# Half of each gated row turned by a DMA transpose, the outer products two steps behind the inner ones

## The reference

```
for _ in range(LOOPS):
    z_norm = _rmsnorm(z, norm_w)
    scores = softmax(z_norm @ router_w)
    topk_vals, topk_idx = top_k(scores, 2)          # 2 of 8 experts, gates normalised to sum 1
    for e in range(E):                              # E = 8, D = 256, F = 512
        h = silu(z_norm @ w1[e]) * (z_norm @ w3[e])
        mixed = mixed + cw[:, e:e+1] * (h @ w2[e])
    z = z + mixed
```

## Time and profile before

| what | value |
|---|---|
| median of three runs | 1050.6 us |
| the profiled execution | 1050.72 us, its span 1049.0 us, mean granted clock 0.989 |
| attention, up to the first tile | about 343 us |
| 142 tiles, gate of the first to gate of the last | 354.70 to 1023.06 us |
| an undisturbed tile | 4.35 us |
| a tile with a combine step beside it | 5.62 us |
| after the last tile's gate | 25.9 us |

### The profile page before, as it was taken

How to read it: one execution, slowest core, us unless ns; L and a number is a source line. 1 busy time by engine, 2 the same in 40 slices (tenths; PEclk the granted TensorE clock), 3 DMA queues, 4 the chain that set the end, 5 groups by cost and what they waited for, 6 DMA issues and landing times.

```text
span 1049.0 us, 22711 instructions
## 1 busy us (share of the span) xinstructions
PE 987.4 (94%) x7246; PEld 678.7 (65%) x7246; DVE 690.5 (66%) x1497; ACT 574.7 (55%) x1122; POOL 579.5 (55%) x755
## 2 busy tenths in 40 slices
PE   7999997989999899999999999999999999999991
...
GB/s 315 370 68 31 38 32 22 1 6 21 15 26 16 67 107 125 87 69 101 91 109 167 132 98 139 88 106 181 112 111 117 96 91 92 170 173 119 143 187 130
DMA packets 153818, 109.26 MB, mean 104 GB/s; under 512 B 100992, under 2 KB 140544, under 8 KB 153728
## 3 DMA queue, kind: packets, MB, share of 16 engines
...
...
## 4 chain that ended last, share of the span: by engine, by line
PE 69%; DVE 9%; POOL 7%; DMA 6%; ACT 4%; issue 3%; SPq 0%; another core or an unknown queue 0%; POOLq 0%; ACTq 0%; DVEq 0%
PE psum_s L930 32%; PE psum_o L2336 16%; PE psum_s L2325 6%; DMA arena<-arena 4%; PE psum_s L1758 3%; PE psum_t L1753 2%; PE psum_t L764 2%; PE psum_o L1804 2%; POOL arena L1057 2%; DVE arena L1489 1%; DMA arena<-in_rope 1%; PE psum_o L1799 1%; PE psum_o L1811 1%; PE psum_s L1735 1%; PE psum_t L2300 1%
## 5 line engine op out<-in xcount | busy, mean ns | idle before, releaser
L930 PE MATMUL psum_s<-w_all,arena 128*128 x1704 | 392.0, 380 | 4.6 <-issue 1.9
L1980 POOL DMA_INDIRECT token_rows<-arena,result_row_of_row x142 | 147.1, 1036 | 296.5 <-ACT arena L2089 291.2
L930 PEld LDWEIGHTS psum_s<-w_all,arena 128*128 128x128 f16 x1704 | 157.8, 98 | 185.2 <-issue 10.9
L2336 PE MATMUL psum_o<-w_all,arena 128*128 x1704 | 209.4, 273 | 9.1 <-DVE arena L2264 8.2
L915 DVE SCALAR_TENSOR_TENSOR arena<-psum_s,gate_scale,arena 128x512 f32<-128x512 f32 x142 | 106.5, 750 | 161.1 <-ACT arena L909 80.6
L2336 PEld LDWEIGHTS psum_o<-w_all,arena 128*128 128x128 f16 x1704 | 164.7, 98 | 54.1 <-issue 15.4
L2264 DVE TENSOR_TENSOR arena<-psum_s,arena 128x512 f16<-128x512 f32 x142 | 97.8, 689 | 132.3 <-ACT arena L2082 114.2
L2089 ACT ACTIVATE arena<-psum_o 128x256 f32<-128x256 f32 x142 | 54.3, 383 | 216.8 <-PE psum_o L2336 214.1
L891 POOL DMA_INDIRECT arena<-sorted_rows,token_of_row x142 | 139.9, 986 | 49.3 <-issue 40.2
L909 ACT ACTIVATE arena<-psum_s,silu_scale 128x512 f32<-128x512 f32 x142 | 97.6, 687 | 108.1 <-PE psum_s L930 56.6
L2082 ACT ACTIVATE arena<-psum_s 128x512 f16<-128x512 f32 x142 | 84.7, 597 | 33.1 <-PE psum_s L2325 22.9
...
## 6 DMA issues: line engine op xcount, KB each, us to landing
...
arena<-sorted_rows,token_of_row POOLq DMA_INDIRECT x142
token_rows<-arena,result_row_of_row POOLq DMA_INDIRECT x142
...
```

The source lines that it names most:

```text
L930: last = nc.tensor.matmul(bank, e_xT[:, u, lx * DC + c, :], w_split[:, bass.ds(e * EW + at, FF)], start=(q == 0), stop=(q == 3 * DC - 1))
L1980: nc.gpsimd.indirect_dma_start(rows, bass.IndirectOffsetOnAxis(ap=targets[:, at : at + 1], axis=0), y_row[:, u, :], None).then_inc(s_sent[ ...
L2336: last = nc.tensor.matmul(psum_e, hT[:, lh, c, :], w_split[:, bass.ds(e * EW + at, D)], start=(q == 0), stop=(q == 3 * FC - 1))
```

## The change

- The gated row is now made in two halves (`gate`, two operations of 256 columns, the second half of the columns first). The first half is turned by TensorE as before, with two transposes in place of four. The second half is split in the row layout (`half_hi` on ScalarE, `half_lo` on VectorE) into the single buffer `h_split`, and turned by a DMA transpose from SyncE's queue (`turn_half`) into one of two buffers, `hT[1]` or `hT[2]`.
- `outer` stands two steps behind: in step n TensorE does the first half of `inner(n)`, `turn_h(n-1)`, the second half of `inner(n)`, work beside, and `outer(n-2)`. With it `h_hi`, `h_lo`, `y_copy` and `send` are those of n-2.
- The first half of the turned row has one PSUM bank and one buffer, `hT[0]`. So `turn_h(n)` waits for `h_lo(n-1)`, and `h_hi(n-1)` waits for `outer(n-2)`.
- On ScalarE `half_hi(n)` stands behind the work beside the tile and ahead of `y_copy(n-2)`; `h_hi(n-1)` and `silu(n+1)` follow.
- `x_pair` and `y_row` have two buffers in place of three, and `plans` moves most beside work of passes 1 to 3 by one step. One of the closing sums that stood beside a tile (`SUMMED` 6 to 4 tiles of rows) now stands behind the last tile.

The diff, cut to its core:

```diff
@@ -791,12 +791,13 @@
         z_early = [take(2 * D)]
         assert used[0] <= tab_at, used[0]
         used[0] = tab_at
-        x_pair = take(UNROLL * D).bitcast(F16).rearrange("p (u l d) -> p u l d", u=UNROLL, l=2)
+        x_pair = take(2 * D).bitcast(F16).rearrange("p (u l d) -> p u l d", u=2, l=2)
         e_xT = take(UNROLL * D).bitcast(F16).rearrange("p (u g t) -> p u g t", u=UNROLL, g=2 * DC)
         silu_a = take(FF)
         h_row = take(FF)
-        hT = take(2 * FF // 2).bitcast(F16).rearrange("p (l c t) -> p l c t", l=2, c=FC)
-        y_row = take(UNROLL * D).rearrange("p (u d) -> p u d", u=UNROLL)
+        hT = [take(FF // 2).bitcast(F16).rearrange("p (l c t) -> p l c t", l=2, c=FC // 2) for _ in range(3)]
+        y_row = take(2 * D).rearrange("p (u d) -> p u d", u=2)
+        h_split = take(FF // 2).bitcast(F16).rearrange("p (l c) -> p l c", l=2)
...
         LAST = ((0, 4), (4, 8), (8, 12), (12, 14), (14, NT))
-        LAST_LOAD, LAST_SUM = LOW_DONE + 2, LOW_DONE + 4
+        LAST_LOAD, LAST_SUM = LOW_DONE + 3, LOW_DONE + 5
         SUMMED = 2 * (MIXED - 1 - LAST_SUM)
-        assert 3072 <= routing_words and SUMMED == 6 and LOW == 12
+        assert 3072 <= routing_words and SUMMED == 4 and LOW == 12
...
         plans = (Plan(None, 3, None, 12, 13, 13, 14, 23, 15, 16, 17, 18, 19, 20, (0,) * 18 + (1, 0, 0, 3), 3, 22),
-                 Plan(16, 18, 26, 27, 28, 29, 30, 31, 32, 33, 34, 35, 36, 36, (0,) * 37 + (1, 1, 1, 1), 27, 41),
-                 Plan(1, 3, 11, 12, 13, 13, 14, 23, 15, 16, 17, 18, 19, 20, (0,) * 18 + (1, 0, 0, 3), 12, 22),
-                 Plan(16, 18, 26, *(None,) * 14))
-        OUT = 29
+                 Plan(17, 19, 27, 28, 29, 30, 31, 32, 33, 34, 35, 36, 37, 37, (0,) * 38 + (1, 1, 1, 1), 28, 42),
+                 Plan(2, 4, 12, 13, 14, 14, 15, 24, 16, 17, 18, 19, 20, 21, (0,) * 19 + (1, 0, 0, 3), 13, 23),
+                 Plan(17, 19, 27, *(None,) * 14))
+        OUT = 30
...
             if n >= UNROLL:
                 sp.wait_ge(s_b, n - UNROLL + 1)
-            sp.dma_start(e_xT[:, u, :, :], x_pair[:, u, :, :].rearrange("p l d -> p (l d)"),
+            sp.dma_start(e_xT[:, u, :, :], x_pair[:, n % 2, :, :].rearrange("p l d -> p (l d)"),
                          transpose=True).then_inc(s_turned[u], 16)
 
         def silu(act, s):
 
             act.wait_ge(s_a, s + 1)
+            if s:
+                act.wait_ge(s_h, s)
             nc.scalar.activation(silu_a, psum_a, ACT.Silu, scale=silu_scale[:, 0:1]).then_inc(s_silu, 1)
 
         def gate(dve, s):
 
             dve.wait_ge(s_b, s + 1)
             dve.wait_ge(s_silu, s + 1)
-            nc.vector.scalar_tensor_tensor(h_row, psum_b, gate_scale[:, 0:1], silu_a, ALU.mult,
-                                           ALU.mult).then_inc(s_h, 1)
+            if s:
+                dve.wait_ge(s_half_lo, s)
+            for half, signal in ((slice(FF // 2, FF), s_gated), (slice(0, FF // 2), s_h)):
+                if s and signal is s_h:
+                    dve.wait_ge(s_th, s)
+                nc.vector.scalar_tensor_tensor(h_row[:, half], psum_b[:, half], gate_scale[:, 0:1], silu_a[:, half], ALU.mult,
+                                               ALU.mult).then_inc(signal, 1)
 
         def expert(pe, k, t):
             at = column(k, t)
@@ -924,6 +936,10 @@
             u = n % UNROLL
             if m == 0:
                 pe.wait_ge(s_turned[u], 16 * (n // UNROLL + 1))
+                if n:
+                    pe.wait_ge(s_silu, n)
+            elif n:
+                pe.wait_ge(s_h, n)
             bank, signal = ((psum_a, s_a), (psum_b, s_b))[m]
             for q, (c, lx, lw) in enumerate([(c, a, w) for c in range(DC) for a, w in ((0, 0), (1, 0), (0, 1))]):
                 at = ((m * DC + c) * 2 + lw) * GROUP
...
@@ -1930,9 +1947,23 @@
                     sp.dma_start(last_results[p][:, :, c, :],
                                  token_rows[at : at + 2 * P, :].rearrange("(g p) d -> p g d", p=P)).then_inc(s_tok[p], 16)
 
+            def turn_half(n):
+
+                sp.wait_ge(s_half_lo, n + 1)
+                if n >= 2:
+                    sp.wait_ge(s_e, n - 1)
+                sp.dma_start(hT[1 + n % 2].rearrange("p l c t -> p (l c) t"), h_split.rearrange("p l c -> p (l c)"),
+                             transpose=True).then_inc(s_half_T, 16)
+
             for k, plan in enumerate(plans):
                 for t in range(PASS[k]):
-                    turn_rows(sp, FIRST[k] + t + 2)
+                    n = FIRST[k] + t
+                    late = plan.index is not None and k % B == 0
+                    if late and t >= PASS[k] - 2:
+                        turn_rows(sp, n + 2)
+                    if not (late and PASS[k] - 3 <= t < PASS[k] - 1):
+                        turn_rows(sp, n + 3)
+                    turn_half(n)
                     if k == END and t == LAST_LOAD:
                         for u in range(UNROLL):
                             sp.wait_ge(s_sent[u], landed(u, FIRST[k] + LOW_DONE))
...
@@ -2079,27 +2111,38 @@
 
             def h_hi(s):
                 act.wait_ge(s_th, s + 1)
-                nc.scalar.activation(hT[:, 0, :, :].rearrange("p c t -> p (c t)"), psum_h, ACT.Copy).then_inc(s_h_hi, 1)
+                if s:
+                    act.wait_ge(s_e, s)
+                nc.scalar.activation(hT[0][:, 0, :, :].rearrange("p c t -> p (c t)"), psum_h[:, 0 : FF // 2],
+                                     ACT.Copy).then_inc(s_h_hi, 1)
+
+            def half_hi(n):
+                act.wait_ge(s_gated, n + 1)
+                if n:
+                    act.wait_ge(s_half_T, 16 * n)
+                nc.scalar.activation(h_split[:, 0, :], h_row[:, FF // 2 :], ACT.Copy).then_inc(s_half_hi, 1)
 
             def y_copy(n):
-                u = n % UNROLL
                 act.wait_ge(s_e, n + 1)
-                if n >= UNROLL:
-                    act.wait_ge(s_sent[u], 16 * (n // UNROLL))
-                nc.scalar.activation(y_row[:, u, :], psum_e, ACT.Copy).then_inc(s_yrow, 1)
+                if n >= 2:
+                    act.wait_ge(s_sent[(n - 2) % UNROLL], 16 * ((n - 2) // UNROLL + 1))
+                nc.scalar.activation(y_row[:, n % 2, :], psum_e, ACT.Copy).then_inc(s_yrow, 1)
 
             for k, plan in enumerate(plans):
                 for t in range(PASS[k]):
                     n = FIRST[k] + t
+                    if n >= 2:
+                        h_hi(n - 2)
                     if n:
-                        h_hi(n - 1)
                         silu(act, n)
                     if k < END:
                         beside(k, plan, t)
-                    if n:
-                        y_copy(n - 1)
-            h_hi(ALL - 1)
-            y_copy(ALL - 1)
+                    half_hi(n)
+                    if n >= 2:
+                        y_copy(n - 2)
+            for n in range(ALL - 2, ALL):
+                h_hi(n)
+                y_copy(n)
             for q, (a, b) in enumerate(LAST):
                 act.wait_ge(s_fshift, q + 1)
...
@@ -2261,19 +2304,25 @@
 
             def h_lo(s):
                 dve.wait_ge(s_h_hi, s + 1)
-                nc.vector.tensor_tensor(hT[:, 1, :, :].rearrange("p c t -> p (c t)"), psum_h,
-                                        hT[:, 0, :, :].rearrange("p c t -> p (c t)"), ALU.subtract).then_inc(s_h_lo, 1)
+                nc.vector.tensor_tensor(hT[0][:, 1, :, :].rearrange("p c t -> p (c t)"), psum_h[:, 0 : FF // 2],
+                                        hT[0][:, 0, :, :].rearrange("p c t -> p (c t)"), ALU.subtract).then_inc(s_h_lo, 1)
+
+            def half_lo(n):
+                dve.wait_ge(s_half_hi, n + 1)
+                nc.vector.tensor_tensor(h_split[:, 1, :], h_row[:, FF // 2 :], h_split[:, 0, :], ALU.subtract).then_inc(s_half_lo, 1)
 
             for k, plan in enumerate(plans):
                 for t in range(PASS[k]):
                     n = FIRST[k] + t
-                    if n:
-                        h_lo(n - 1)
+                    if n >= 2:
+                        h_lo(n - 2)
                     gate(dve, n)
...
@@ -2321,7 +2370,9 @@
             def turn_h(n):
 
                 pe.wait_ge(s_h, n + 1)
-                for c in range(FC):
+                if n:
+                    pe.wait_ge(s_h_lo, n)
+                for c in range(FC // 2):
                     last = nc.tensor.transpose(psum_h[:, c * P : (c + 1) * P], h_row[:, c * P : (c + 1) * P], ident[:, :])
                 last.then_inc(s_th, 1)
 
@@ -2331,31 +2382,37 @@
                 if n:
                     pe.wait_ge(s_yrow, n)
                 for q, (c, lh, lw) in enumerate([(c, a, w) for c in range(FC) for a, w in ((0, 0), (1, 0), (0, 1))]):
+                    if q == 3 * FC // 2:
+                        pe.wait_ge(s_half_T, 16 * (n + 1))
                     per = GROUP // D
                     at = ((2 * DC + c // per) * 2 + lw) * GROUP + c % per * D
```

(21 more changed lines are left out.)

35 lines of the change are left out of this document (22 added, 13 removed).

## The result

| | before | changed |
|---|---|---|
| median of 4 runs | 1050.7 us | 1187.7 us (1180.2 to 1192.3) |
| ratio, 95% interval | 1 | 1.130 (1.123 to 1.136) |
| profiled run, its span | 1050.7, 1049.0 | 1180.2, 1178.4 |
| mean granted clock of TensorE | 0.989 | 0.961 |

Slower, as forecast, but by 137 us where 87 were forecast, and outside the range.

A forecast was written before the change was run, and what follows sets the result against it. TensorE's own work (4.35 us a tile) was taken as the bound; the change's new rounds of waits would replace it. Losses summed by stretches, with +5.2 at the end, gave 87.1 us on 1050.7: 1138 us, range 1108 to 1168.

The forecast's parts named there:

- Round D: Chain over VectorE from bank b's end through gate, half_lo, work beside and h_lo to TensorE's matmuls: 3.66 + b us.
- b: VectorE's work beside a tile: its busy time less 1.44 us a tile, times 1.08 in linked routing operations.
- Combine tiles of the fourth pass: The 8 tiles from 905.13, b 2.16 us: 46.6 us in all, +11.6; about 5.8 apart.
- finishing tiles: The fourth pass's 8 tiles from 953.16, b 1.31 us: 39.8 us in all, +4.8; 5.0 a tile.
- The first combine: The 8 tiles from 373.61, b 1.45, half_hi behind copy_zT and two row parts: period 6.58 us, +6.2.
- Round P: Chain over ScalarE from outer's end through y_copy, h_hi, h_lo, transposes and bank b to outer's next end: 4.44 us.
- Costs at nothing: Half's transfer (1.2 us of room), two buffers in x_pair and y_row, and SyncE's extra issue would add no time.
- a rival at 0.10: The half's transfer decides, late behind loads in 24 combine tiles: +62, with half of it 1169 us; chance 0.10.
- 4 us inside the third pass's last routing tiles: In the stretch from 761.25, half_hi waits behind a turn of rows that waits for indices: 0 to 8, 4 taken.
- The clock: TensorE's clock drops to 1.2 GHz after waits over 2 us in 15 tiles, 1.4 each: +21, 1159 us; chance 0.10.
- TensorE as the bound (1012): Rival: turn_h finds h_lo done, the period falls to 4.13 us and stalls go: 1012 us; chance 0.06.
- round P alone (1063): Rival: only the chain over ScalarE binds, VectorE's work finds room: 141 x 0.09 = +13, 1063 us; chance 0.04.

The follow-up runs named there:

- Opening this round alone: Changed kernel with h_lo(n-1) moved on VectorE ahead of the work beside tile n: 1117.9 us, ratio 1.066.
- opening both: Changed kernel with h_lo(n-1) moved ahead of VectorE's work beside and h_hi(n-1) ahead of y_copy(n-2) on ScalarE: 1107.4 us, ratio 1.054.
- filling waits: Changed kernel with 321 idle matmuls, in 38 tiles, into an unused PSUM bank ahead of turn_h: 1169.6 us, ratio 1.118.

## Why the prediction was wrong

**Round D, the bulk of the sum: right.** Combine tiles of the fourth pass were forecast at 5.82 and are 5.85, with b at the same place; finishing tiles 4.97 and 4.93. Opening this round alone gave 67 to 70 us back, opening both 79 to 80, against a forecast of 87 for everything; but these gains hold some of the clock, which the 87 did not. The first combine was too high (6.58 for 6.25).

**Round P: right in its links,** 0.13 high (4.44 for 4.31), the overlap of `h_hi` with `y_copy`.

**"Costs at nothing": this step failed.** "The half's transfer ... 1.2 us of room" holds for a lone transfer. But `h_split` has one buffer, and SyncE's queue carries loads, stores and gathers' turnings ahead of it: 6.8 us to its landing in tile 44, 31 waits of `half_hi` in all. A second buffer is worth 26 us. The other half of the step held: the third buffer of `x_pair` brought nothing when it was given back alone. I had the mechanism as a rival at 0.10 and gave it +31; its size was near, its chance was not. Each term I named against it (a pair is half of four loads, a tile lies between) was about one burst, and the changed kernel has four loads in a row ahead of the half at tiles 44, 115 and 139 (10.62, 9.41 and 9.46 us) and a turning that waits for its gather ahead of it at tiles 1 and 95 (11.91 and 11.44). For the latter the forecast had 4 us inside the third pass's last routing tiles; at tile 95 alone 7.0 came.

**The clock: a rival that came true beside the forecast,** and so a term that the sum had at nothing. +21 was its term, from 15 waits over 2 us; TensorE has 23 such waits ahead of `turn_h`, and filling waits gave 12 to 18 us back. What I set against it, that waits up to 1.7 us had left the clock at 1.00, held in the three stretches at 1.00, whose longest waits are 0.69, 1.61 and 0.62 us. It was no argument for waits longer than that: the longest wait in the stretch at 0.95 is 2.64 us, in that at 0.90 it is 4.35. Nor was the clock an alternative: the rounds make the waits, and the waits cost the clock. Forecast, clock and the buffer's 26 give 1176 to 1182, against 1187.7. That this comes so near is partly luck: the terms overlap (the fill stood in waits that the transfer had made, and the buffer's 26 hold some clock), and the losses of the long tiles were not added up one by one.

**The row stores**, which the prediction did not speak of when it let them go one step later, give 26.6 us of waits of `row_hi`. Moving them back alone changed nothing that can be told: those waits lay beside round D.

**What stays open.** In the routing tiles of the second and third passes the loss was 22.1 for 11.6 and 27.9 for 23.5. The clock (0.93 and 0.90 there) is in it, and the stores' waits stand there; how much is b spread unevenly over tiles, where a sum of means understates a sum of maxima, was not measured apart.

TensorE as the bound (1012) and round P alone (1063) fell with the profile of the changed kernel.
